# A cross-attention and feed-forward layer on one core: five blocks with barriers become one block, written out

## The reference

```python
x = x + xattn(layernorm(x), ctx, pos, pos, Wq, Wkv, Wout, bout)   # 32 heads of 16, axial RoPE, softmax over 512
x = x + ffn(layernorm(x), w_fc, w_proj)
# ffn: h = gelu(bitlinear(x, w_fc)); return bitlinear(h, w_proj)      (2048 hidden features)
# bitlinear(x, w): xn = (x - mean) / sqrt(var + eps); clip xn * 128 / max|xn| to +-128, scale back;
#                  times sign(round(w / mean|w|)) * mean|w|
```

## Time and profile before

| | us |
|---|---|
| median of 3 runs | 890.2 (888.17 to 891.32) |
| the profiled execution | 892.17 |
| its span, first to last instruction | 890.4 |
| PE / DVE / ACT / POOL busy | 825.2 / 711.7 / 460.8 / 362.1 |
| projection, up to the last stores of q and k | 3 to 149 |
| attention | 148.2 to 549 |
| mix | 549 to 655.5 |
| feed-forward | 655.5 to 890.4 |

### The profile page before, as it was taken

How to read it: one execution, slowest core, us unless ns; L and a number is a source line. 1 busy time by engine, 2 the same in 40 slices (tenths; PEclk the granted TensorE clock), 3 DMA queues, 4 the chain that set the end, 5 groups by cost and what they waited for, 6 DMA issues and landing times. The chain is left out here.

```text
span 890.4 us, 15912 instructions
## 1 busy us (share of the span) xinstructions
PE 825.2 (93%) x4290; PEld 367.5 (41%) x4290; DVE 711.7 (80%) x970; ACT 460.8 (52%) x873; POOL 362.1 (41%) x512
## 2 busy tenths in 40 slices
PE   1899995999999999999999997999669999999996
PEld 0788882232333333333333322565324444444442
DVE  4888875888888888888888852799949999998892
ACT  3576662377777777777777775233333112122110
POOL 2488876544444444444444420677711111011010
PEclk9999996599999999999999999999969999999998
DMA  7378886333332333343223202343004365454363
GB/s 250 99 207 246 238 228 152 95 96 97 86 85 79 95 95 84 95 95 93 81 78 93 83 1 76 113 142 94 13 1 73 81 119 107 83 106 100 76 119 83
DMA packets 136134, 94.36 MB, mean 106 GB/s; under 512 B 77088, under 2 KB 116000, under 8 KB 136096
## 3 DMA queue, kind: packets, MB, share of 16 engines
q1 hardware_dynamic: 136096, 93.90, 42.2%
HBM read 55.85 MB, written 16.78 MB: 82 GB/s over the span
## 5 line engine op out<-in xcount | busy, mean ns | idle before, releaser
L771 DVE TENSOR_REDUCE attend_maxima<-attend_banks 128x2 f32<-128x1024 f32 x256 | 301.7, 1220 | 64.9 <-PE attend_banks L696 64.7
L794 ACT ACTIVATE attend_probs<-attend_banks 128x512 f32<-128x512 f32 x512 | 271.9, 596 | 84.7 <-PE attend_banks L728 84.7
L728 PE MATMUL attend_banks<-stacks_q_stack,stacks_k_stack 98*128 98x512 bf16 x512 | 175.6, 386 | 2.0 <-ACT attend_probs L794 1.8
L696 PE MATMUL attend_banks<-stacks_k_stack,stacks_q_stack 96*128 96x512 bf16 x512 | 161.1, 398 | 6.8 <-PEq L151 4.5
L738 PE MATMUL attend_banks<-attend_probs,attend_v_ones 128*32 128x512 f32 x1024 | 137.3, 608 | 1.5 <-ACT attend_probs L794 1.0
L1252 ACT ACTIVATE kept_o_all<-ffn_banks,kept_row_scale 128x512 f32<-128x512 f32 x64 | 44.0, 687 | 147.6 <-PE ffn_banks L1217 139.4
L1230 PE MATMUL ffn_banks<-kept_wT,kept_o_all 128*128 128x512 f16 x512 | 115.3, 385 | 4.8 <-DMA kept_o_all<-kept_o_all 4.8
L1217 PE MATMUL ffn_banks<-kept_wT,kept_uT 128*128 128x512 f16 x512 | 114.8, 384 | 1.4 <-PEq L870 1.4
L728 PEld LDWEIGHTS attend_banks<-stacks_q_stack,stacks_k_stack 98*128 98x128 bf16 x512 | 39.5, 97 | 140.5 <-ACT attend_probs L794 85.5
L1331 POOL TENSOR_SCALAR ffn_powers<-ffn_moments 128x1 f32<-128x1 f32 x16 | 17.5, 1091 | 180.4 <-DVE ffn_moments L1269 180.4
L829 POOL TENSOR_SCALAR attend_neg_max<-attend_maxima 128x16 f32<-128x16 f32 x32 | 8.3, 259 | 188.5 <-DVE attend_maxima L771 188.5
(11 more groups left out here) (147 smaller groups left out, 1091.9 us busy)
## 6 DMA issues: line engine op xcount, KB each, us to landing
k_parts<-kept_wT SPq DMA_DIRECT2D x48, 128.0 KB, 3.0
q_parts<-kept_wT SPq DMA_DIRECT2D x48, 128.0 KB, 2.4
stacks_q_stack<-q_parts SPq DMA_DIRECT2D x32, 192.0 KB, 3.0
stacks_k_stack<-k_parts SPq DMA_DIRECT2D x96, 64.0 KB, 2.6
stacks_k_stack<-k_parts SPq DMA_DIRECT2D x32, 192.0 KB, 2.7
kept_o_all<-in_x_dram SPq DMA_DIRECT2D x16, 256.0 KB, 3.4
kept_o_all<-in_L_ffn_w_fc_dram SPq DMA_DIRECT2D x16, 256.0 KB, 3.2
kept_o_all<-in_L_ffn_w_proj_dram SPq DMA_DIRECT2D x16, 256.0 KB, 5.1
```

Of the source, the lines that this page charges most:

```text
L696: mm = nc.tensor.matmul(score_slot[j % 2][:, i], q_stack[0:STACK, slot, head, c * P:(c + 1) * P], k_stack[0:STACK, slot, head, :], start=T ...
L728: nc.tensor.matmul(banks[:, ST_BANK[k]], k_stack[0:STACK + 2, slot, head, c * P:(c + 1) * P], q_stack[0:STACK + 2, slot, head, :], start=T ...
L771: dve.tensor_reduce(maxima[:, at.slot(2), 2 * j:2 * j + 2], score_slot[j % 2], AX.X, ALU.max).then_inc(scores_read, 1)
L794: nc.scalar.activation(probs[:, c, head, :], banks[:, ST_BANK[k]], ACT.Exp, scale=1 / math.sqrt(HEAD)).then_inc(exp_done, 1)
```

## The change

All five blocks become one, without a barrier between stages and without hardware loops: every step is written out. Each engine goes on to the next stage when its list gets there. The memory is laid out once, and stages share regions of it. Beyond that:

- **v through DRAM.** ACT writes each tile's v into `v_pad`, 32 columns a head with ones in the upper 16. `store_v` stores it (512 KB in pieces of 512 B, 16 times), `load_v` loads 256 KB a group into a ring of three. POOL's copies of v (L822) go.
- **First stacks.** Four groups' stacks and three of v are loaded during the projection (two stacks before).
- **Attention's start.** Its first step is woven into the projection's last on PE and DVE.
- **Weights.** The ternary pieces are turned by DMA (`turn_weight`), so the four transposes (L709) and ACT's copy (L803) go.
- **Softmax sums.** ACT, not DVE, saves numerators and sums, to a ring of three. `store_sums` stores each group to DRAM, and `load_sums` loads a pair of groups back with the features on partitions, numerators in one tile, each head's sum repeated over 16 partitions in another. DVE inverts a whole 128x512 tile a pair (`invert_sums`, 16 in all: 13 in the steps of the groups, between reductions 3 and 4 of every second group, and 3 after), POOL multiplies (`divide`). All transposes on PE in mix go, and with them L991, L997 and ACT's copies.
- **Rows.** mix and feed-forward run in one pipeline. PE's step s is expand(s), mix(s+2), contract(s-2). DVE's is in the diff. u is turned by DMA, the mean of h is subtracted by ACT (`centre_h`) in place of DVE, and the order around it is new.

The diff replaces nearly every line. Its core, with the functions that are new:

```diff
--- before.py
+++ after.py
...
-def project(nc, x, ctx, pos, wq, wkv, w_fc, w_proj, ident, spare, wT, v_all, gammas, limits, q_parts, k_parts,
...
-def attend(nc, w_fc, w_proj, identb, ident16, limits, v_all, q_parts, k_parts, q_stack, k_stack,
...
-def mix(nc, x, wout, bout, ident, ident16, o_all, gammas, x1, uT, row_scale):
...
-def ffn(nc, o_all, uT, row_scale, gammas, x1, wT, out):
...
+    def store_v(self, sp, n):
+        sp.wait_ge(self.v_saved, n + 1)
+        sp.dma_start(self.mem.v_padded.rearrange("b g p c e -> b c p g e")[n // CHUNKS, n % CHUNKS],
+                     self.v_pad[:, n % 2].rearrange("p (g e) -> p g e", g=HG)).then_inc(self.v_stored[n % 2], DMA)
...
+        need(sp, self.pv_done, (g - V_SLOTS + 1) * CHUNKS)
+        sp.dma_start(self.mem.v_ones[:, g % V_SLOTS].rearrange("p c h e -> p c (h e)"),
+                     self.mem.v_padded[g // HG, g % HG]).then_inc(self.v_loaded[g % V_SLOTS], DMA)
...
+    def turn_weight(self, sp, n):
+        sp.wait_ge(self.ternary_ready, n + 1)
+        sp.dma_start_transpose(self.mem.wT[:, n].rearrange("p (k r) -> p k r", k=KX), self.ternary[:, n % 2]
+                               ).then_inc(self.wT_turned[n % 2], DMA)
...
+    def store_sums(self, sp, g):
+        sp.wait_ge(self.o_saved, g + 1)
+        sp.dma_start(self.mem.o_rows[g], self.o_ring[:, g % O_SLOTS]).then_inc(self.o_stored[g % O_SLOTS], DMA)
...
+    def load_sums(self, sp, pair):
+        for g in (2 * pair, 2 * pair + 1):
+            sp.wait_ge(self.o_stored[g % O_SLOTS], (g // O_SLOTS + 1) * DMA)
...
+        rows = self.mem.o_rows[2 * pair:2 * pair + 2].rearrange("g (j t d) q -> t (g j) d q", t=2, d=HEAD)
+        for to, t in ((self.numer, 0), (self.sums, 1)):
+            sp.dma_start(to[:, pair % 2], rows[t]).then_inc(self.sums_loaded[pair % 2], DMA)
...
+    def invert_sums(self, dve, pair):
+        r = pair % 2
+        dve.wait_ge(self.sums_loaded[r], (pair // 2 + 1) * 2 * DMA)
+        dve.reciprocal(self.sums[:, r], self.sums[:, r]).then_inc(self.inverted, 1)
...
+    def save_sums(self, act, g):
+        need(act, self.o_stored[g % O_SLOTS], g // O_SLOTS * DMA)
+        act.wait_ge(self.pv_done, (g + 1) * CHUNKS)
+        act.copy(self.o_ring[:, g % O_SLOTS], self.pv_bank).then_inc(self.o_saved, 1)
...
+    def divide(self, pool, pair):
+        pool.wait_ge(self.inverted, pair + 1)
+        pool.tensor_tensor(self.attnT[:, pair], self.numer[:, pair % 2], self.sums[:, pair % 2], ALU.mult
+                           ).then_inc(self.divided, 1)
...
+    def turn_u(self, sp, n):
+        sp.wait_ge(self.u_ready, n + 1)
+        need(sp, self.fc_ready, (n - U_SLOTS + 1) * QUARTERS)
+        sp.dma_start_transpose(self.uT[:, n % U_SLOTS], self.u_parts[:, n % 2].rearrange("p t c -> p (t c)")
+                               ).then_inc(self.u_turned[n % U_SLOTS], DMA)
...
+        c = n % CHUNKS
+        for k in range(KX):
+            mm = self.nc.tensor.matmul(self.y_bank[n % 2], att.attnT[:, n // CHUNKS * KX + k, c * P:(c + 1) * P],
+                                       self.wout_sb[:, k, :], start=(k == 0), stop=(k == KX - 1))
+        mm.then_inc(self.mix_ready, 1)
...
+        need(dve, self.out_scale_ready, n)
+        dve.tensor_reduce(scale(0), now, AX.X, ALU.max, apply_absolute_value=True).then_inc(self.h_step, 1)
+        dve.wait_ge(self.h_step, n * 5 + 1)
+        dve.reciprocal(scale(1), scale(0)).then_inc(self.h_step, 1)
+        dve.wait_ge(self.h_step, n * 5 + 2)
+        dve.tensor_scalar(scale(2), scale(1), -Q_B, None, ALU.mult).then_inc(self.h_step, 1)
...
+        dve.wait_ge(self.h_step, n * 5 + 4)
+        dve.tensor_scalar(now, now, scale(2), Q_B, ALU.mult, ALU.min).then_inc(self.h_step, 1)
...
+        dve.wait_ge(self.h_step, n * 5 + 5)
+        dve.tensor_scalar(self.h_parts[:, r, 0], now, -Q_B, None, ALU.max).then_inc(self.h_first, 1)
...
+        dve.scalar_tensor_tensor(self.h_parts[:, r, 1], now, -Q_B, self.h_parts[:, r, 0], ALU.max, ALU.subtract
+                                 ).then_inc(self.parts_ready, 1)
...
+    def centre_h(self, act, n):
+        act.wait_ge(self.h_stats_ready, n + 1)
+        now = self.h[:, n % H_SLOTS, :]
+        act.activation(now, now, ACT.Identity, bias=self.h_moments[:, n % 2, 0:1], scale=-1.0
+                       ).then_inc(self.h_centred, 1)
...
+                if within(s - 2, TILES):
+                    prj.load_piece(sp, w_fc, w_proj, s - 2)
+                if within(s - 4, TILES):
+                    prj.store_v(sp, s - 4)
+                if within(s - 5, TILES) and (s - 5) % 2 == 1:
+                    prj.store_parts(sp, s - 5)
+                if 12 <= s < 16:
+                    att.load_stacks(sp, s - 12)
+                if 13 <= s < 16:
+                    att.load_v(sp, s - 13)
...
+            for s in range(GROUPS + 5):
+                if s < GROUPS:
+                    att.load_weight(sp, w_fc, w_proj, s)
+                if STACK_SLOTS <= s < GROUPS:
+                    att.load_stacks(sp, s)
+                if within(s - 4, GROUPS):
+                    att.store_sums(sp, s - 4)
+                if within(s - 5, GROUPS) and (s - 5) % 2 == 1:
+                    att.load_sums(sp, (s - 5) // 2)
+                if within(s - 2, GROUPS):
+                    att.load_max(sp, s - 2)
+                if V_SLOTS <= s - 1 < GROUPS:
+                    att.load_v(sp, s - 1)
+                if within(s - 2, GROUPS):
+                    att.turn_weight(sp, s - 2)
+                if s == 8:
+                    rows.load_weights(sp, wout, bout)
+                if 9 <= s < 11:
+                    rows.load_x(sp, x, s - 9)
+                if s == GROUPS + 2:
+                    rows.load_x(sp, x, 2)
+                    rows.turn_u(sp, 0)
...
+            for s in range(TILES + 3):
+                if 3 <= s + 3 < TILES:
+                    rows.load_x(sp, x, s + 3)
+                if within(s - 1, TILES):
+                    rows.turn_h(sp, s - 1, 0)
+                if s + 1 < TILES:
+                    rows.turn_u(sp, s + 1)
+                if within(s - 1, TILES):
+                    rows.turn_h(sp, s - 1, 1)
+                if within(s - 3, TILES):
+                    rows.store(sp, out, s - 3)
...
+            att.scores(pe, 0, 0)
+            prj.turn_rotated(pe, TILES - 1, 0)
+            att.scores(pe, 0, 1)
+            prj.turn_rotated(pe, TILES - 1, 1)
+            att.scores(pe, 0, 2)
+            prj.add_totals(pe)
+            for j in range(3, 2 * GH):
+                att.scores(pe, 0, j)
+
+            for s in range(1, GROUPS + 3):
+                att.tensor_step(pe, s)
+                if s in (GROUPS, GROUPS + 1):
+                    rows.mix(pe, s - GROUPS)
...
+            for s in range(TILES + 2):
+                if s < TILES:
+                    for o in range(QUARTERS):
+                        rows.expand(pe, s, o)
+                if s + 2 < TILES:
+                    rows.mix(pe, s + 2)
+                if within(s - 2, TILES):
+                    rows.contract(pe, s - 2)
...
+            prj.sum_ffn(dve)
+            prj.rope_products(dve, TILES - 1, 1)
+            att.row_maxima(dve, 0, 0)
+            prj.take_first(dve, TILES - 1, 0)
+            att.row_maxima(dve, 0, 1)
+            prj.take_first(dve, TILES - 1, 1)
+            att.row_maxima(dve, 0, 2)
+            prj.weigh_ffn(dve)
+            for j in range(3, 2 * GH):
+                att.row_maxima(dve, 0, j)
+            dve.wait_ge(prj.gamma_step, 4)
+            dve.tensor_scalar(rows.gamma_128[:], mem.gammas[:], 1 / Q_B, None, ALU.mult).then_inc(rows.gamma_set, 1)
+
+            for s in range(1, GROUPS):
+                for j in range(2 * GH):
+                    if j == 4 and s >= 6 and s % 2 == 0:
+                        att.invert_sums(dve, (s - 6) // 2)
+                    att.row_maxima(dve, s, j)
+            dve.wait_ge(rows.gamma_set, 1)
+            att.invert_sums(dve, PAIRS - 3)
+            rows.add_residual(dve, 0)
+            att.invert_sums(dve, PAIRS - 2)
+            rows.quantise_u(dve, 0)
+            rows.add_residual(dve, 1)
+            att.invert_sums(dve, PAIRS - 1)
...
+            for s in range(TILES + 3):
+                if within(s - 3, TILES):
+                    rows.finish(dve, s - 3)
+                if 2 <= s + 1 < TILES:
+                    rows.add_residual(dve, s + 1)
+                if within(s - 1, TILES):
+                    rows.clip_h(dve, s - 1)
+                if s < TILES:
+                    rows.statistics(dve, s, 0)
+                    rows.statistics(dve, s, 1)
+                if s + 1 < TILES:
+                    rows.quantise_u(dve, s + 1)
+                if s < TILES:
+                    rows.statistics(dve, s, 2)
+                    rows.statistics(dve, s, 3)
+                    rows.join_statistics(dve, s)
+                if within(s - 1, TILES):
+                    rows.second_h(dve, s - 1)
...
```

(26 more changed lines are left out.)

1964 lines of the change are left out of this document (889 added, 1075 removed).

## The result

The changed kernel takes 919.0 us (median of 4 runs, 918.5 to 921.0), the kernel before 889.7 in the same comparison: a ratio of 1.033, 95% interval 1.031 to 1.036. It is slower by 29 us; 881 was forecast. The profiled execution has a span of 917.2 us. Of the 35.6 us between that and the forecast sum of 881.6, 6.8 lie ahead of the first turned score, 26.6 between it and the last exponential, and 2.2 behind.

A forecast was written before the change was run, and what follows sets the result against it. PE was taken to bound the attention and the rows, DMA the end of the projection. Span 890.4 + 11.3 (ramp) + 25.9 (attention) - 46.0 (rows) = 881.6 us; forecast 881 us, range 848 to 904.

The forecast's parts named there:

- rival F: Attention: a stall of 2.56 us drops TensorE's clock, some 5 us more each, 65 in all: 946 us; chance 0.10.
- Reciprocals: Attention, between reductions 3 and 4: 128x512 inversion takes 3.3 us, PE stands 2.56 us, 13 times, +33.3 us.
- rival C: Attention: the reciprocal is short, as any pass of 512, so no stall: 848 us; chance 0.08.
- D: Attention: the reciprocal is long, 4.3 us or more; a stall of 3.6 gives 895 us; chance 0.12.
- Transposes: Attention: the four transposes (L709) leave PE 32 times, 0.23 us each time: -7.4 us.
- The attention's account: Whole attention: -7.4 us for transposes and +33.3 for stalls behind reciprocals, +25.9 us in sum.
- Ramp: Projection and attention's start: DMA work 158 us, 16 idle, last parts stored at 174.5, first turned score at 178.4, +11.3 us.
- rival B: Projection: the v stores are hidden, -17.3 us, 864 us; chance 0.18.
- A: The forecast itself, whole kernel: 868 to 893 us with its own terms off by a few us; chance 0.37.
- Rows: Mix and feed-forward: PE-bound steps of 17.26 us, 297.3 us from last exponential to end, now 343.3: -46.0 us.
- rival E: Rows: the loop through u is longer than PE's work, 18.3 us a step, 896 us; chance 0.15.

## Why the prediction was wrong, point by point

**The step that failed** is this: "ACT swaps a copy of 512 columns for another one and has 0.7 us of slack a quarter. POOL's work stays under its step. I cost both at nothing; PE's list covers them." ACT has the time. But the copy had also moved, from ahead of DVE's second reduction to behind ACT's fifth exponential, and its place decides when the one PSUM bank of `weigh_v` is free: 31 waits, 23.1 us. The list of changes named the move from DVE to ACT, and I asked what the copy costs its engine, not who waits for it. Putting this right alone would not have saved the forecast. With the copy early the kernel took 911.4 us, since each stall then took the clock down (rival F). And the other 12.5 of the 35.6 us, in the points below, make 894 of the forecast's sum, still slower than before.

- *Reciprocals.* Right in place and size: 3.34 us (3.3 forecast; the line through both rows gives 3.38), a stall of 2.34 (2.56), 30.4 us in 13 (33.3). The estimate from the Trainium skill's repeat count of 8 ("VectorE: DVE Perf Modes", First, the fixed hardware budget) was 4.3 us; the line through the two shorter rows was nearer. Neither rival C nor D was it.
- *Transposes.* L709 is gone, -7.4, in the account below.
- *The attention's account.* 380.0 us before, 432.5 after: -7.4 + 30.4 + 23.1, and 3.6 for mix(0), which PE's list has ahead of the last step's products; I had left it out there. Of the 2.8 left, 1.5 are the half speed behind the first stall: from its end to the second's it takes 28.8 us, between the others 27.3. The remaining 1.3 I have not traced.
- *Rival F, the clock.* False for the changed kernel but for one stall of 13. It was one edit away: with the copy early, or in the kernel before, the same reciprocal takes the clock down each time. Its price was some 1.5 us a stall with the copy early. In the kernel before it was 1.7 behind 11 stalls and 4.8 behind four, so the 5 that I took is what the long ones cost.
- *Ramp.* The last parts came when forecast, on two errors that cancel: 152 us of DMA work up to 175 us, not 158, and 23 us idle, not 16. By the run with half of v a store is 1.5 to 1.7 us, an estimate from two shares, between the row's 2.3 and the 1.2 that I estimated from the best rate in the Trainium skill ("DMA: Bandwidth & Descriptors", Specifications). So rival B was false, and the v stores cost less than in A. Behind the parts I was 6.8 short: 2.3 for POOL's order, which I had not followed through its queue, and 4.5 mostly for reductions that "end near 165 to 172" by my text and ended at 174 for group 0 alone.
- *Rows.* 299.5 us (297.3), in part by errors that cancel. The first expansion starts 8.8 us behind the last exponential (7.5, where the three terms named add up to 7.2). The third starts 32.1 behind the first (27.5), since the sums' inversion waits 9 us for its DMA. Against that the step behind the third is 2.6 us short of the sum's, which had put the slow clock there. The step is 17.25 us (17.26) twelve times, `centre_h` 2.0 (2.2), and PE is the bound as forecast. With the order put back, some 1.0 us more in the loop of u, the steady step did not grow, so the room was there, and rival E was false. What I had not seen is that the same 1.0 us costs most of 7.6 us at the start and the end of the rows, where PE does wait for u.
- *What would have shown it wrong* said "if PE doesn't wait for the reciprocals, if the stores of v don't delay the last parts, or if PE has gaps in the rows' steps". All three went as forecast; the miss was in a part costed at nothing. Only the length of the groups gave it away: 12.4 and 14.9 us in turn, where the list has 11.6 and 14.2.

## What to carry to other kernels

When a copy out of PSUM changes its engine, look for who waits for the bank, and place the copy where its data are complete: one number in a loop (k = 1 in place of 4) decided 26 us once the stalls were gone. A long operation on an engine that paces PE is to be cut into pieces that fit its slack. What a wait costs depends on the waits beside it (7.6 or 26 us for the same copy), so take them away together before judging one. A step moved on one engine gains nothing while the DMA queue keeps its order; here it cost 5 us until the queue's order moved with it. And count a shift from the event that releases it: the last parts came at 167.4 and at 164.6 us in two kernels with the same start.

## What was not expected of the hardware

- The same stall of 2.34 us leaves the clock at 1.00 in 12 of 13 cases in the changed kernel, where PE also waits 0.72 us for the copy in each group, and takes it to half for 3.4 us in 13 of 13 where that wait is gone. In the kernel before, stalls of 2.11 us took it down 15 of 15 times, 11 times for 3.4 us and four times for 10.2. Two stalls of 0.74 and 0.94 us in a group leave it up. Taking a wait away can so cost nearly what it gives. What decides it stays open. The wait for the copy alone doesn't: it stood ahead of the changed kernel's first stall too, and the clock fell behind that. When exactly a stall comes may count as well as the work ahead of it, and no run varied either alone.
- The reciprocal goes by elements from 64 to 512: 534, 1740 and 3344 ns for 64, 256 and 512 columns, so 6.3 ns for each more.
